# Transposes of a local-attention kernel in 64-token row tiles of the array, in place of 128x128

## The chip, the core and the metric

One core of one Trainium2 chip runs the program. TensorE (PE, with its weight loads listed as PEld), VectorE (DVE), ScalarE (ACT) and GpSimd (POOL) work at once and wait for each other through semaphores. The metric is device time in microseconds (us), the median of some runs.

## The reference

All arithmetic is float32. The input is x, 16 batches of 128 tokens with 128 features. A cross-attention block comes first. Then, for each of two layers, a local attention with 8 heads of 64 and a gated feed-forward part follow:

```python
h = shift_token(x)
q, k, v = split(h @ wqkv, 3)
q = l2norm(q) * qs;  k = l2norm(k) * ksc
q, k = rotary_xpos(q, k)
o = local_attention(q, k, v)     # window 64, looks one window back
x = x + o @ wo
h = layernorm(shift_token(x)) * lg + lb
h = h @ w1 + b1
a, g = split(h, 2)
x = x + (a * gelu(g)) @ w2 + b2
```

Since 128 tokens are two windows, the attention of a batch is a dense 128x128 score matrix of each head under one mask.

## The kernel before, in words

The change lies in the attention of the two layers. There the residual is kept transposed (features on partitions) in `xs`. A batch passes these steps:

- PE projects q, k and v (`qkv`, L386), each one 128x512 product into its own bank of PSUM. ACT squares q and k (L668), DVE sums the squares (L978), ACT turns them into factors (L672, L674). DVE multiplies by the rotary tables (L968, L971), POOL adds the two halves (L347) and scales k (L354). q and k of the batch now lie in `cs`, tokens on partitions.
- `rows_T` (L515): PE transposes q in four 128x128 pieces into bank TQ, and k in four into bank TK (L521). Each piece holds two heads. ACT copies bank TQ to `qT` (`q_rows`, L770), DVE copies bank TK to `kT` (`k_rows`, L997).
- `scores_` (L525): eight products with 64 rows each (L535), the two heads of a pair in the two halves of the array's rows.
- DVE applies factor and mask and finds the negated maxima (`maxima_`, L986, begun by a small MEMSET at L257 that waits for the scores), ACT takes the exponentials (`weights`, L757), DVE the reciprocals (L993), and POOL divides (L340). Even heads (a=0) and odd heads (a=1) are separate halves throughout.
- `weights_T` (L538): PE transposes the four weight matrices of a half, again into TQ (a=0) or TK (a=1) (L546). ACT copies each half to `pT` (`weights_out`, L762).
- `attend` (L549): products with v (L559), ACT copies the result (`heads_out`, L766), PE multiplies by wo (`out_proj`, L566), DVE adds it to `xs` (L1008), PE subtracts the mean (`deviation`, L571), ACT squares (L774), PE averages (`variance`, L575), ACT forms the factor (L778, L780) and DVE writes the normalised row (L1012).

The batches are software-pipelined by hand. `pipeline` calls on each engine a function `step`, in which at(d) is the batch n+d. The order of the calls in each `step` is the order in the engine's queue, and each engine works its queue in that order. In one step PE handles v and the transposes of batch n+2, the output product of batch n, q of batch n+4, mean and variance of batch n, the scores of n+2, the weight transposes and the attention product of n+1, and k of n+5. The weight transposes of the even half stand before `variance`, those of the odd half after the scores. In the same step ACT does the exponentials of n+1 with the copy of the heads of n between their halves, then the q copy of n+2, squares of k, the small functions, the copy of the even weights, squares of q, and the copy of the odd weights.

An fp32 product is two passes of the array, and so counts as two instructions in the trace; a transpose is one.

## Time and profile before

| | us |
|---|---|
| median of 3 runs (451.48 to 452.88) | 452.82 |
| span of the profiled execution | 452.5 |
| PE busy | 391.6 |
| DVE busy | 342.2 |
| ACT busy | 299.5 |
| POOL busy | 205.4 |

The profiled execution gives only its span, from the first to the last instruction; its own time outside the span isn't recorded. The span lies 0.3 us below the median of the runs. Busy times are sums over the whole span, which holds the cross-attention, two attention stages of 16 batches each and two feed-forward parts. The change touches the attention stages alone, so the views below are cut to them. Matmul ends are modelled, and neighbouring matmuls overlap, so that a busy PE isn't PE at its peak.

### The profile page before, as it was taken

What the parts mean: (1) busy time and instruction counts of PE and PEld (TensorE: products, weight loads), DVE (VectorE), ACT (ScalarE), POOL (GpSimd) and SP (SyncE); (2) the same over time, 40 slices, a digit from 0 to 9 for tenths busy, and PEclk for the clock granted to TensorE, in tenths of its full rate; (3) what the DMA queues carried; (4) which work ended last, traced back from release to release, by engine and by line L of the source; (5) the groups of instructions that cost most, each with busy time, mean ns of one, the idle gap of its engine ahead of it and who ended that gap; (6) DMA issues with size and microseconds to landing.
All of it is one profiled execution on the core that took longest, in us unless ns stands there. A gap on an engine that the chain in (4) does not pass through costs nothing.

```text
span 452.5 us, 8032 instructions
## 1 busy us (share of the span) xinstructions
PE 391.6 (87%) x2504; PEld 258.5 (57%) x2504; DVE 342.2 (76%) x1308; ACT 299.5 (66%) x986; POOL 205.4 (45%) x229
## 2 busy tenths in 40 slices
PE   0678677799999999987789888999999999867995
PEld 0456552477777767765434345767767777654442
DVE  2688747899999999984135689999999999612345
ACT  2355533589899899886432338889898998653224
POOL 6261103585775766762000066767757757410000
PEclk9988985999999999999989989999999999967898
DMA  7920000000000000000000000000000000000003
GB/s 158 292 55 2 1 1 0 0 3 1 1 2 2 0 2 1 3 0 1 0 1 0 1 0 2 0 3 2 2 0 1 3 1 1 2 1 0 0 0 93
DMA packets 10263, 7.25 MB, mean 16 GB/s; under 512 B 3245, under 2 KB 9431, under 8 KB 10222
## 3 DMA queue, kind: packets, MB, share of 16 engines
q1 hardware_dynamic: 8590, 5.63, 4.6%
q0 software_dynamic: 832, 1.12, 1.3%
q8 instruction: 20, 0.33, 0.3%
q14 instruction: 21, 0.17, 0.1%
q10 hardware_dynamic: 800, 0.00, 0.1%
HBM read 5.70 MB, written 1.05 MB: 15 GB/s over the span
## 4 chain that ended last, share of the span: by engine, by line
DVE 56%; PE 31%; issue 6%; ACT 4%; DMA 1%; SPq 0%; DVEq 0%; ACTq 0%
DVE pp L986 11%; PE ps L511 10%; DVE shared L971 8%; DVE ss L978 8%; DVE shared L968 7%; PE ps L618 5%; DVE kT L997 4%; PE ps L386 3%; DVE vv L1001 3%; DVE xs L1008 2%; PE ps L566 2%; PE ps L535 1%; DVE pri L993 1%; DVE nm L986 1%; DVE shared L872 1%
## 5 line engine op out<-in xcount | busy, mean ns | idle before, releaser
L386 PE MATMUL ps<-wqkv_raw,xs 128*128 128x512 f32 x192 | 108.2, 652 | 11.1 <-DVE shared L971 11.1
L340 POOL TENSOR_TENSOR pp<-pp,pri 128x512 f32<-128x512 f32 x64 | 66.6, 1041 | 94.8 <-DVE pri L993 94.8
L757 ACT ACTIVATE pp<-pp,nm 128x128 f32<-128x128 f32 x256 | 99.2, 389 | 10.3 <-DVE nm L986 10.3
L347 POOL TENSOR_TENSOR shared<-shared 128x512 f32<-128x512 f32 x64 | 81.4, 1275 | 0.0
L986 DVE CUSTOM_DVE_ANT_0 pp<-ps,msk,rr 128x128 f32<-128x128 f32 x256 | 72.4, 347 | 0.0
L511 PE MATMUL ps<-hn,w1g 128*128 128x512 f32 (+1 forms) x96 | 49.4, 637 | 5.8 <-DVE uu L1063 5.8
L757 ACT ACTIVATION_READ_ACCUMULATOR pp<-pp,nm 128x1 f32 x256 | 48.1, 188 | 0.0
L971 DVE TENSOR_TENSOR shared<-ps,stab 128x256 f32<-128x256 f32 x128 | 47.6, 413 | 0.0
L386 PEld LDWEIGHTS ps<-wqkv_raw,xs 128*128 128x128 f32 x192 | 31.1, 200 | 27.0 <-DVE shared L971 17.7
L968 DVE TENSOR_TENSOR shared<-ps,ctab 128x512 f32<-128x512 f32 x64 | 42.9, 671 | 2.5 <-ACT sqr L668 2.4
L559 PEld LDWEIGHTS ps<-pT,vv 128*64 128x64 f32 x512 | 28.2, 139 | 26.9 <-issue 24.1
L668 ACT ACTIVATE sqr<-ps 128x512 f32<-128x512 f32 x64 | 37.5, 586 | 8.7 <-PE ps L386 8.6
L1063 DVE SCALAR_TENSOR_TENSOR uu<-ps,b_all,gl 128x512 f32<-128x512 f32 (+1 forms) x24 | 17.6, 748 | 33.4 <-ACT gl L825 33.4
L978 DVE TENSOR_REDUCE ss<-sqr 128x8 f32<-128x512 f32 x64 | 40.7, 677 | 1.5 <-ACT sqr L668 1.5
L559 PE MATMUL ps<-pT,vv 128*64 128x128 f32 x512 | 35.9, 283 | 6.8 <-ACT pT L762 6.8
L546 PE MATMUL ps<-idn,pp 128*128 128x128 f32 x256 | 41.0, 284 | 0.1
L521 PEld LDWEIGHTS ps<-idn,shared 128*128 128x128 f32 x256 | 31.0, 141 | 17.3 <-issue 17.3
L825 ACT ACTIVATE gl<-ps,b_all 128x512 f32<-128x512 f32 (+1 forms) x24 | 16.0, 685 | 37.2 <-PE ps L511 37.2
L762 ACT ACTIVATE pT<-ps 128x512 f32<-128x512 f32 x64 | 37.5, 589 | 4.4 <-PE ps L546 4.4
L359 POOL TENSOR_SCALAR ssc<-ss 128x16 f32<-128x16 f32 x32 | 7.9, 246 | 69.6 <-DVE ss L978 69.6
L566 PE MATMUL ps<-oT,wo_raw 128*128 128x128 f32 x256 | 36.2, 287 | 3.6 <-ACT oT L766 3.6
L521 PE MATMUL ps<-idn,shared 128*128 128x128 f32 x256 | 37.7, 273 | 0.0
(118 smaller groups left out, 673.1 us busy)
## 6 DMA issues: line engine op xcount, KB each, us to landing
wqkv_raw<-in_L_ffn_wqkv_dram SPq DMA_DIRECT2D x1, 1536.0 KB, 16.4
out_dram<-shared SPq DMA_DIRECT2D x4, 256.0 KB, 2.5
w_raw<-in_L_ffn_w_dram SPq DMA_DIRECT2D x1, 682.0 KB
xt<-in_x_dram SPq DMA_DIRECT2D x2, 256.0 KB, 4.5
xt<-in_x_dram SPq DMA_DIRECT2D x1, 512.0 KB, 12.4
wo_raw<-in_L_ffn_wo_dram SPq DMA_DIRECT2D x1, 512.0 KB
ct<-in_ctx_dram POOLq DMA_DIRECT2D x1, 360.0 KB, 12.2
w_raw<-in_L_ffn_w_dram SPq DMA_DIRECT2D x2, 128.0 KB
```

What stands on the lines that cost most here:

```text
L340: T(pp[m.j][:, a, :, :], pp[m.j][:, a, :, :], pri[m.j][:, a * 4:a * 4 + 4].unsqueeze(2).to_broadcast([128, PAIRS, 128]), ALU.mult).then_in ...
L347: T(cs[m.j][:, part], cs[m.j][:, part], sn[m.j][:, part], ALU.add).then_inc((aq_done, ak_done)[s], 1)
L386: mm(ps[:, part, :], xs[:, m.b, 0:N], wqkv_raw[:, m.layer, part * INNER:(part + 1) * INNER], start=True, stop=True).then_inc((q_ps, k_ps, ...
L511: last = mm(ps[0:m, 2 * c + s, :], w1g[:, layer, o2:o2 + m], hg, start=True, stop=True)
L521: last = tr(ps[:, TQ + s, c * 128:(c + 1) * 128], cs[m.j][:, s * INNER + c * 128:s * INNER + (c + 1) * 128], idn[:])
L559: last = mm(ps[a * 64:a * 64 + 64, OB, c * 128:(c + 1) * 128], vv[m.j][:, h * DH:(h + 1) * DH], pT[m.j][:, a, c, :], start=True, stop=True)
L566: last = mm(ps[:, OB, Y], wo_raw[:, m.layer, c, :], oT[m.j][:, c, :], start=(c == 0), stop=(c == PAIRS - 1))
L757: A(pp[m.j][:, a, c, :], pp[m.j][:, a, c, :], ACT.Exp, bias=nm[m.j][:, a * 4 + c:a * 4 + c + 1], scale=-1.0, accum_out=psum_[m.j][:, a * 4 ...
L968: V.tensor_tensor(heads(cs[m.j], s), x_, ctab[:, m.layer, s, :].unsqueeze(1).to_broadcast([128, HEADS, DH]), ALU.mult)
L971: last = V.tensor_tensor(heads(sn[m.j], s)[:, :, o_], x_[:, :, i_], stab[:, m.layer, s, o_].unsqueeze(1).to_broadcast([128, HEADS, 32]), A ...
L978: V.tensor_reduce(ss[m.j][:, s * HEADS:(s + 1) * HEADS], heads(sqr[m.j], s), AX.X, ALU.add).then_inc(sq_sum, 1)
L986: last = V.tensor_tensor_reduce(out=pp[m.j][:, a, c, :], in0=ps[:, SA + a, c * 128:(c + 1) * 128], in1=msk[:], scale=rr[m.j][:, h:h + 1], ...
```

## The change

Each 128x128 transpose becomes two transposes of 64 tokens: one reads partitions 0 to 63, the other partitions 64 to 127 of the same piece (`row_tiles`). They use the two halves of the array's rows, and each writes 128x64 values: tokens 0 to 63 go to bank TQ, tokens 64 to 127 to bank TK. A bank thus holds no longer q or k (or even or odd heads), but one half of the tokens of all eight pieces. So:

- `rows_T` transposes q and k of a batch in one go of 16 instructions, after `out_proj`. It waits for both q and k from POOL. `q_rows` on ACT copies the lower tokens of q and k to the new tile `rT`, `k_rows` on DVE the upper ones. Both wait for the one semaphore `rT_ps`.
- `weights_T` transposes all eight weight matrices in one go of 16 instructions, after the scores. It waits for both halves from POOL. Both copies of `weights_out` wait for the one semaphore `pt_ps`.
- The copies write with a stride: eight runs of 64 values each.

```diff
--- before.py
+++ after.py
@@ -156,12 +156,12 @@
         cut = Carve()
         (cs0, sn0), (cs1, sn1) = ([cut(N, 2 * INNER) for _ in range(2)] for _ in range(2))
         cs, sn = (cs0, cs1), (sn0, sn1)
-        qT, kT = sb2("qT", [128, PAIRS, N]), sb2("kT", [128, PAIRS, N])
+        rT = sb2("rT", [128, 2 * PAIRS, N])
         vv = sb2("vv", [N, INNER])
         pp = [sb(f"pp{k}", [128, 2, PAIRS, 128]) for k in range(2)]
         zo = pp[1][:, 0, :, :]
         nm, psum_, pri = (sb2(n, [128, HEADS]) for n in ("nm", "psum_", "pri"))
-        pT = [sb(f"pT{k}", [128, 2, PAIRS, 128]) for k in range(2)]
+        pT = sb2("pT", [128, 2 * PAIRS, 128])
         oT = sb2("oT", [128, PAIRS, N])
         dsq, lnl, rstd = (sb(n, [D, N]) for n in ("dsq", "lnl", "rstd"))
 
@@ -202,10 +202,11 @@
         sqq_done, sqk_done, sq_sum, ss_ready, ln_done, r_ready = (
             sem(n) for n in ("sqq_done", "sqk_done", "sq_sum", "ss_ready", "ln_done", "r_ready"))
         tq_done, tk_done, aq_done, ak_done, mk_done = (sem(n) for n in ("tq_done", "tk_done", "aq_done", "ak_done", "mk_done"))
-        qT_ps, kT_ps, qT_ready, kT_ready, v_ready = (sem(n) for n in ("qT_ps", "kT_ps", "qT_ready", "kT_ready", "v_ready"))
+        rT_ps, lo_ready, hi_ready, v_ready = (sem(n) for n in ("rT_ps", "lo_ready", "hi_ready", "v_ready"))
         s_ps = sem("s_ps")
-        nm_done, p_done, ri_ready, pn_ready, pt_ps, pt_ready = (
-            sem2(n) for n in ("nm_done", "p_done", "ri_ready", "pn_ready", "pt_ps", "pt_ready"))
+        pt_ps = sem("pt_ps")
+        nm_done, p_done, ri_ready, pn_ready, pt_ready = (
+            sem2(n) for n in ("nm_done", "p_done", "ri_ready", "pn_ready", "pt_ready"))
         o_ps, oT_ready, y_ps, x_upd = (sem(n) for n in ("o_ps", "oT_ready", "y_ps", "x_upd"))
         m_ps, d2_ready, var_ps, lnl_done, rstd_ready, hn_ready = (
             sem(n) for n in ("m_ps", "d2_ready", "var_ps", "lnl_done", "rstd_ready", "hn_ready"))
@@ -512,39 +513,46 @@
                 if 1 in halves_:
                     last.then_inc(g_ps[c], 1)
 
-            def rows_T(m, s):
+            def row_tiles(t, bank, done):
+
+                for c in range(2 * PAIRS):
+                    for u, r in enumerate((slice(0, 64), slice(64, 128))):
+                        last = tr(ps[:, bank + u, c * 64:c * 64 + 64], t(c)[r, :], idn[r, r])
+                last.then_inc(done, 1)
+
+            def rows_T(m):
 
                 if m.b >= 2:
-                    pe.wait_ge(pt_ready[s], m.i - 1)
-                pe.wait_ge((aq_done, mk_done)[s], m.i + 1)
-                for c in range(PAIRS):
-                    last = tr(ps[:, TQ + s, c * 128:(c + 1) * 128],
-                              cs[m.j][:, s * INNER + c * 128:s * INNER + (c + 1) * 128], idn[:])
-                last.then_inc((qT_ps, kT_ps)[s], 1)
+                    pe.wait_ge(pt_ready[0], m.i - 1)
+                    pe.wait_ge(pt_ready[1], m.i - 1)
+                pe.wait_ge(aq_done, m.i + 1)
+                pe.wait_ge(mk_done, m.i + 1)
+                row_tiles(lambda c: cs[m.j][:, c * 128:(c + 1) * 128], TQ, rT_ps)
 
             def scores_(m):
 
-                pe.wait_ge(qT_ready, m.i + 1)
-                pe.wait_ge(kT_ready, m.i + 1)
+                pe.wait_ge(lo_ready, m.i + 1)
+                pe.wait_ge(hi_ready, m.i + 1)
                 if m.b > 0:
                     pe.wait_ge(nm_done[0], m.i)
                     pe.wait_ge(nm_done[1], m.i)
                 for c in range(PAIRS):
                     for a in range(2):
                         r = slice(a * 64, a * 64 + 64)
-                        last = mm(ps[:, SA + a, c * 128:(c + 1) * 128], qT[m.j][r, c, :], kT[m.j][r, c, :], start=True, stop=True)
+                        last = mm(ps[:, SA + a, c * 128:(c + 1) * 128], rT[m.j][r, c, :], rT[m.j][r, PAIRS + c, :], start=True, stop=True)
                 last.then_inc(s_ps, 1)
 
-            def weights_T(m, a):
+            def weights_T(m):
 
                 if m.b + 1 < B:
-                    pe.wait_ge((qT_ready, kT_ready)[a], m.i + 2)
-                else:
-                    pe.wait_ge(pt_ready[a], m.i)
-                pe.wait_ge(pn_ready[a], m.i + 1)
-                for c in range(PAIRS):
-                    last = tr(ps[:, TQ + a, c * 128:(c + 1) * 128], pp[m.j][:, a, c, :], idn[:])
-                last.then_inc(pt_ps[a], 1)
+                    pe.wait_ge(lo_ready, m.i + 2)
+                    pe.wait_ge(hi_ready, m.i + 2)
+                elif m.i > 0:
+                    pe.wait_ge(pt_ready[0], m.i)
+                    pe.wait_ge(pt_ready[1], m.i)
+                pe.wait_ge(pn_ready[0], m.i + 1)
+                pe.wait_ge(pn_ready[1], m.i + 1)
+                row_tiles(lambda c: pp[m.j][:, c // PAIRS, c % PAIRS, :], TQ, pt_ps)
 
             def attend(m):
 
@@ -557,7 +565,7 @@
                     for a in range(2):
                         h = 2 * c + a
                         last = mm(ps[a * 64:a * 64 + 64, OB, c * 128:(c + 1) * 128], vv[m.j][:, h * DH:(h + 1) * DH],
-                                  pT[m.j][:, a, c, :], start=True, stop=True)
+                                  pT[m.j][:, a * PAIRS + c, :], start=True, stop=True)
                 last.then_inc(o_ps, 1)
 
             def out_proj(m):
@@ -577,11 +585,10 @@
             def step(at, on):
                 if on(2):
                     project_v(at(2))
-                    rows_T(at(2), 0)
                 if on(0):
                     out_proj(at(0))
                 if on(2):
-                    rows_T(at(2), 1)
+                    rows_T(at(2))
                 if on(4):
                     project_q(at(4))
                 if on(0) and at(0).b == B - 3:
@@ -594,8 +601,6 @@
                     hidden(at(0).layer, 0, 1)
                 if on(0):
                     deviation(at(0))
-                if on(1):
-                    weights_T(at(1), 0)
                 if on(0) and not on(1):
                     hidden(at(0).layer, 0, 2, [0])
                 if on(0):
@@ -603,7 +608,7 @@
                 if on(2):
                     scores_(at(2))
                 if on(1):
-                    weights_T(at(1), 1)
+                    weights_T(at(1))
                 if on(5):
                     project_k(at(5))
                 if on(1):
@@ -758,16 +763,16 @@
                       scale=-1.0, accum_out=psum_[m.j][:, a * 4 + c:a * 4 + c + 1]).then_inc(p_done[a], 1)
 
             def weights_out(m, a):
-                act.wait_ge(pt_ps[a], m.i + 1)
-                A(pT[m.j][:, a, :, :].rearrange("p c n -> p (c n)"), ps[:, TQ + a, :], ACT.Copy).then_inc(pt_ready[a], 1)
+                act.wait_ge(pt_ps, m.i + 1)
+                A(pT[m.j][:, :, a * 64:a * 64 + 64], ps[:, TQ + a, :].rearrange("p (c n) -> p c n", n=64), ACT.Copy).then_inc(pt_ready[a], 1)
 
             def heads_out(m):
                 act.wait_ge(o_ps, m.i + 1)
                 A(oT[m.j][:].rearrange("p c n -> p (c n)"), ps[:, OB, :], ACT.Copy).then_inc(oT_ready, 1)
 
             def q_rows(m):
-                act.wait_ge(qT_ps, m.i + 1)
-                A(qT[m.j][:].rearrange("p c n -> p (c n)"), ps[:, TQ, :], ACT.Copy).then_inc(qT_ready, 1)
+                act.wait_ge(rT_ps, m.i + 1)
+                A(rT[m.j][:, :, 0:64], ps[:, TQ, :].rearrange("p (c n) -> p c n", n=64), ACT.Copy).then_inc(lo_ready, 1)
 
             def dev_square(m):
                 act.wait_ge(m_ps, m.i + 1)
@@ -963,7 +968,7 @@
 
                 dve.wait_ge((sqq_done, sqk_done)[s], m.i + 1)
                 if s == 1 and m.i >= 2:
-                    dve.wait_ge(kT_ps, m.i - 1)
+                    dve.wait_ge(rT_ps, m.i - 1)
                 x_, done = ps[:, QB + s, :].rearrange("p (h d) -> p h d", d=DH), (tq_done, tk_done)[s]
                 V.tensor_tensor(heads(cs[m.j], s), x_, ctab[:, m.layer, s, :].unsqueeze(1).to_broadcast([128, HEADS, DH]), ALU.mult)
                 for u in range(2):
@@ -993,8 +998,8 @@
                 V.reciprocal(pri[m.j][:, a * 4:a * 4 + 4], psum_[m.j][:, a * 4:a * 4 + 4]).then_inc(ri_ready[a], 1)
 
             def k_rows(m):
-                dve.wait_ge(kT_ps, m.i + 1)
-                V.tensor_copy(kT[m.j][:].rearrange("p c n -> p (c n)"), ps[:, TK, :]).then_inc(kT_ready, 1)
+                dve.wait_ge(rT_ps, m.i + 1)
+                V.tensor_copy(rT[m.j][:, :, 64:128], ps[:, TK, :].rearrange("p (c n) -> p c n", n=64)).then_inc(hi_ready, 1)
 
             def v_rows(m):
                 dve.wait_ge(v_ps, m.i + 1)
```

The first queue shown is that of PE, one step in the middle of an attention stage. `cs` is a part of the tile `shared`, and a product stands here as one row. Before:

```order
L386 MATMUL ps<-wqkv_raw,xs 128x512
L521 MATMUL ps<-idn,shared 128x128 x4
L566 MATMUL ps<-oT,wo_raw 128x128 x4
L521 MATMUL ps<-idn,shared 128x128 x4
L386 MATMUL ps<-wqkv_raw,xs 128x512
L571 MATMUL ps<-xs,cen 128x128
L546 MATMUL ps<-idn,pp 128x128 x4
L575 MATMUL ps<-dsq,ones 128x128
L535 MATMUL ps<-kT,qT 128x128 x8
L546 MATMUL ps<-idn,pp 128x128 x4
L386 MATMUL ps<-wqkv_raw,xs 128x512
L559 MATMUL ps<-pT,vv 64x128 x8
```

And the same step of PE now:

```order
L387 MATMUL ps<-wqkv_raw,xs 128x512
L574 MATMUL ps<-oT,wo_raw 128x128 x4
L520 MATMUL ps<-idn,shared 128x64 x16
L387 MATMUL ps<-wqkv_raw,xs 128x512
L579 MATMUL ps<-xs,cen 128x128
L583 MATMUL ps<-dsq,ones 128x128
L542 MATMUL ps<-rT 128x128 x8
L520 MATMUL ps<-idn,pp 128x64 x16
L387 MATMUL ps<-wqkv_raw,xs 128x512
L567 MATMUL ps<-pT,vv 64x128 x8
```

The q transposes moved from ahead of the output product (L566, now L574) to behind it, and the even weight transposes from ahead of the variance product (L575, now L583) to behind the scores.

The second queue is that of ACT, from the small functions of one step to the first exponentials of the next. Before:

```order
L778 ACTIVATE lnl<-ps,epst 128x128 [waits var_ps]
L780 ACTIVATE rstd<-lnl 128x128 [waits lnl_done]
L762 ACTIVATE pT<-ps 128x512 [waits pt_ps0]
L668 ACTIVATE sqr<-ps 128x512 [waits q_ps]
L762 ACTIVATE pT<-ps 128x512 [waits pt_ps1]
L757 ACTIVATE pp,psum<-pp,nm 128x128 [waits nm_done0]
```

And the same stretch of ACT now:

```order
L783 ACTIVATE lnl<-ps,epst 128x128 [waits var_ps]
L785 ACTIVATE rstd<-lnl 128x128 [waits lnl_done]
L767 ACTIVATE pT<-ps 128x8x64 [waits pt_ps]
L673 ACTIVATE sqr<-ps 128x512 [waits q_ps]
L767 ACTIVATE pT<-ps 128x8x64 [waits pt_ps]
L762 ACTIVATE pp,psum<-pp,nm 128x128 [waits nm_done0]
```

The order of ACT is the same. What the first copy waits for has changed: `pt_ps0` came with the even weight transposes ahead of the scores, `pt_ps` comes with all of them behind the scores.

## Rows read from the trace of the kernel before

**Rows 1.** The page, part 4: shares by engine of the chain that ended last.
```profile
DVE 56%; PE 31%; issue 6%; ACT 4%; DMA 1%; SPq 0%; DVEq 0%; ACTq 0%
```

**Rows 2.** Busy time by stretch: length, PE, PEld, DVE, ACT, POOL, clock, DMA share.
```profile
124.00:204.00 80.00, 78.18 (x635) 56.66 (x635) 77.64 (x319) 72.12 (x259) 55.38 (x58) 1.00 0.01 2
150.73:159.05 8.32, 8.32 (x68) 5.98 (x67) 8.22 (x33) 7.56 (x28) 5.76 (x7) 1.00 0.00 0
...
400.00:412.00 12.00, 9.60 (x40) 7.26 (x41) 1.63 (x6) 2.53 (x6) 1.04 (x1) 0.51 0.00 1
```

**Rows 3.** Timeline of one step: start, length in us, engine, line, operation, count.
```profile
150.73 0.06 DVE L257 MEMSET mark_v<- 128x1 f32 x1
...
151.98 0.40 ACT L757 ACTIVATE pp<-pp,nm 128x128 f32<-128x128 f32 x1 [0.18 <-DVE nm L986]
...
153.54 0.57 ACT L766 ACTIVATE oT<-ps 128x512 f32<-128x512 f32 x1
...
154.38 1.06 PE L566 MATMUL ps<-oT,wo_raw 128*128 128x128 f32 x8
...
155.27 0.60 PE L521 MATMUL ps<-idn,shared 128*128 128x128 f32 x4
...
155.47 0.61 DVE L1008 TENSOR_TENSOR xs<-ps,xs 64x128 f32<-64x128 f32 x2
155.56 0.57 ACT L770 ACTIVATE qT<-ps 128x512 f32<-128x512 f32 x1
...
155.71 1.03 PE L386 MATMUL ps<-wqkv_raw,xs 128*128 128x512 f32 x2
156.03 0.58 ACT L668 ACTIVATE sqr<-ps 128x512 f32<-128x512 f32 x1
...
156.57 0.38 PE L571 MATMUL ps<-xs,cen 128*128 128x128 f32 x2
...
156.99 0.28 ACT L774 ACTIVATE dsq<-ps 128x128 f32<-128x128 f32 x1 [0.38 <-PE ps L571]
...
157.32 0.49 PE L575 MATMUL ps<-dsq,ones 128*128 128x128 f32 x2
...
157.74 1.16 PE L535 MATMUL ps<-kT,qT 64*128 64x128 f32 x16
...
158.25 0.31 ACT L780 ACTIVATE rstd<-lnl 128x128 f32<-128x128 f32 x1
158.47 0.58 ACT L762 ACTIVATE pT<-ps 128x512 f32<-128x512 f32 x1
158.77 0.28 DVE L1012 TENSOR_TENSOR hn<-ps,rstd 128x128 f32<-128x128 f32 x1
...
158.84 0.66 PE L546 MATMUL ps<-idn,pp 128*128 128x128 f32 x4
...
159.05 0.06 DVE L257 MEMSET mark_v<- 128x1 f32 x1
...
159.33 1.02 PE L386 MATMUL ps<-wqkv_raw,xs 128*128 128x512 f32 x2
...
159.53 0.60 ACT L762 ACTIVATE pT<-ps 128x512 f32<-128x512 f32 x1
```

**Rows 4.** Instructions of a line, 124 to 204 us: ns least/median/most, first and last start.
```profile
L546 PE MATMUL ps<-idn,pp x77: 272/273/328, 123.8 to 200.5; 128*128 128x128 f32 x77
...
L535 PE MATMUL ps<-kT,qT x160: 272/272/373, 124.5 to 200.0; 64*128 64x128 f32 x160
...
L546 PEld LDWEIGHTS ps<-idn,pp x76: 137/141/146, 125.5 to 200.4; 128*128 128x128 f32 x76
...
L535 PEld LDWEIGHTS ps<-kT,qT x160: 182/188/188, 124.4 to 199.8; 64*128 64x128 f32 x160
```

**Rows 5.** The same view of the 16 normalised rows of each layer.
```profile
L1012 DVE TENSOR_TENSOR hn<-ps,rstd x16: 277/278/292, 100.2 to 224.8; 128x128 f32<-128x128 f32 x16
...
L1012 DVE TENSOR_TENSOR hn<-ps,rstd x16: 276/278/292, 285.2 to 414.5; 128x128 f32<-128x128 f32 x16
```

## The prediction

> **What bounds the kernel now.** Start with the chain that ended last. It gives 56% to DVE and 31% to PE, hardly any to ACT [rows 1]. That suggests DVE as the bound, so read the busy times of a stretch in the middle of an attention stage next. In 80 us PE is busy 78.18, DVE 77.64, ACT 72.12, and the granted clock is 1.00, the 2.4 GHz level [rows 2]. Two engines are full and the third nearly so. Which of them sets the pace can't be told from sums, so take one step in order of time [rows 3]. I count it from one MEMSET mark_v to the next, 150.73 to 159.05, 8.32 us. This MEMSET is the DVE instruction that waits for the scores.
>
> The timeline shows a ring that passes through all three engines. Scores end at 157.74+1.16 = 158.90, DVE starts at 159.05. DVE's first maxima release the first exponential of ACT, 1.25 us behind the MEMSET (151.98), and ACT did wait there (0.18, released by DVE). The copy of the heads follows on ACT at 153.54. It ends at 154.11 and releases the output product (154.38). PE then works through k transposes (155.27), q of a later batch (155.71) and deviation (156.57). ACT's square waits for it (0.38 idle, start 156.99). The variance (157.32) waits for the square, and the scores (157.74) follow it. In between, DVE's addition to the residual starts at 155.47, just when the output product ends (154.38+1.06 = 155.44).
>
> So the step is a ring with little slack anywhere. The important sign for this change is where the copies of the transposed weights stand on ACT. The even one starts at 158.47, before the scores are done. The odd one starts at 159.53, 0.48 behind the MEMSET, and is the last thing on ACT ahead of the exponentials.
>
> **The price of a pair of row tiles.** Full transposes follow each other in (0.60-0.27)/3 = 0.109 us (L521 at 155.27). The new ones stream 64 columns instead of 128, so 0.055 for a pair if both halves of the array work at once and the weight load hides. That halves do work at once is seen in the scores: 16 passes of 64 rows in 1.16 us, of which 0.10 is a long first pass (373 ns against 272, rows 4), so (1.16-0.27-0.10)/7 = 0.112 per pair, as much as one full pass. Whether 128 weight columns load in 0.055 has to be bounded. After a switch the first pass is as much longer as its weights take to load: 373-272 = 0.101 us for the scores, but 328-273 = 0.055 for a transpose. The loads' own durations say the same (188 against 141 ns) [rows 4]. So load and stream would just match, and the upper end is 0.109, if they can't overlap or if instructions can't be issued at twice the rate. I take 0.06, near the lower end because of the 0.055 row, and keep 0.109 for the range.
>
> The Trainium skill (TensorE: Matmul & The Clock Gate, LDWEIGHTS) gives a load as the weight columns divided by 1.2 GHz, whatever the number of rows: 107 ns for 128 columns, so halving the rows would save nothing and a pair would cost as much as a full transpose. The trace agrees for the scores (0.101) and disagrees for transposes (0.055). By the rule the second rival below would be the forecast.
>
> **The price of changing between row tiles and the full array.** The variance ends at 157.32+0.49 = 157.81, so its last pass started at 157.54. The first scores start at 157.74 and are 0.10 long, so in effect at 157.84, 0.30 behind. Without a change the next pass follows after 0.11 (q's at 155.71 behind k's last). A change therefore costs 0.20 where full weights load, and behind the scores, where the last pair starts at 158.90-0.27 = 158.63 and the transposes in effect at 158.84+0.055 = 158.90, it costs 0.16. A transpose next to a product of the same tiling costs nothing extra, as the 154.38 to 155.71 stretch shows. The Trainium skill (TensorEngine Tiling (Array Packing), Key Properties) states that a change of mode drains TensorE. The trace agrees, with these 0.16 to 0.20 us.
>
> **The change part by part, along the ring of one step.**
> 1. Weight transposes and ACT. All 16 stand behind the scores now. They start 0.11 behind the scores' last pair (same tiling, no change): 158.74. The last of 8 pairs starts at 158.74+7x0.06 = 159.16 and ends at 159.43. ACT follows 0.03 after an end of PE, as DVE did at 155.47: 159.46. This is the first copy, which before was at 158.47, under cover of the scores. The spacing of such a copy to the next operation is 0.47 (155.56 to 156.03), and the squares of q stand between the two copies, so the second copy is at 159.46+0.94 = 160.40 and the exponentials can start at 160.87. That is 1.82 behind the MEMSET, against 1.25 to 1.30 before: I take +0.54. DVE's maxima were late; now ACT itself is late. The copies' stride costs nothing in my sum: there is no row of it in this stage, and I allow 0.1 us each for the range.
> 2. Output product. It follows the copy of the heads, so +0.54. Before, the q transposes held it up: heads done 154.11, output product at 154.38. After a wait for ACT a product starts in effect 0.16 behind (square done 157.27, variance at 157.32 plus a 0.10 longer first pass). So it could have started 0.10 earlier, and moving q away gives that back: +0.44.
> 3. Output product to q. Before, 155.71-154.38 = 1.33. Now 8 passes of 0.112 = 0.89, a change 0.16, 8 pairs 0.48, a change back 0.20: 1.73, so +0.40. Halving the transposes' time is eaten here by the two changes and by q's four, which were off the ring.
> 4. From q to the next MEMSET. The even weight transposes no longer stand between deviation and variance, but they were hidden behind ACT's square (156.99 to 157.27, variance at 157.32): 0.
> 5. The copies of q and k. Both wait for the last pair. With q's projection at 155.71+0.84 = 156.55, that pair starts 0.26 before (0.06 + 0.20) at 156.29 and ends at 156.56. ACT copies at 156.59 and squares until about 157.6. The square of the deviation is due at 156.99+0.84 = 157.83, so it hides, with 0.2 to spare. On DVE the residual comes 0.44 later and the k copy also waits for the last pair, some 0.05 more. DVE's last normalised row would be ready at 158.77+0.5 = 159.27, but waits for its factor (158.56+0.84 = 159.40, row at 159.43). It takes 0.28, and the scores come at 159.05+0.84 = 159.89 for DVE: hidden.
> 6. PE behind the weight transposes. k's projection follows at 159.16+0.06+0.20 = 159.42, 0.1 later than before, and attention waits for the second copy, done at 160.40+0.60 = 161.0. PE idles some 0.8 us, but the heads are copied by ACT only in its order, at 160.87+1.56: hidden, as attention, 16 passes like the scores' 1.16 us, ends by 162.4.
>
> Sum: 0.44+0.40 = 0.84 us per step, 8.32 to 9.16. A layer has 14 steps with both an output product and new scores. I count 13, because at a layer's start the ring isn't closed yet. 26 x 0.84 = 21.8 us. The profiled span of 452.5 would become 474.3. It lies 0.3 below the median of the runs, 452.82, so 474.6; I say 475.
>
> **The rivals.**
> - Pairs cost 0.109. Then term 3 grows by 8x0.049 = 0.39 and term 1 by 7x0.049 = 0.34: 0.73 more per step, 19 us, so 494. For it: no row shows two loads and two passes in less than 0.109. Against: the 0.055 load after a switch.
> - PE has the last word and the change is no slower. PE is busy in all 8.32 us of the step [rows 2]. It gives up 16x0.109 = 1.74 and takes 16x0.06 = 0.96, and changes cost +0.16+0.20 around rows and -0.16+0.20 around weights: 0.38 less. DVE has 8.22 busy in a step, so at most 0.1 could be had: -2.6, 450. The place is ACT's first exponential. If it starts within 1.3 us of the MEMSET the ring isn't lengthened there. That needs both weight copies ready 0.5 us earlier than I find. Against: ACT works in order, and its first copy can't start before the scores end.
> - The clock falls. PE gets holes of 0.8 us, and in the sparse end of the second layer the clock was 0.51, the 1.2 GHz level, while the same stretch of the first layer kept it. That layer took 414.5-285.2 = 129.3 us against 124.6 [rows 5]: 4.7 us for one such fall [rows 2]. Two of them on top of the forecast: 484. Against: PE would still be busy some nine tenths of each step.
>
> **How the numbers follow.** Forecast 0.66: 475, own range 466 to 484 (a change that costs nothing between transposes and products takes off 0.2 to 0.36 a step, up to 9 us; strides or a pair of 0.075 add as much). Pairs at 0.109: 0.18, at 494. Clock: 0.09, at 484. PE's rival: 0.05, at 450. Rest 0.02. To hold 8 in 10 the range takes the forecast's own, the clock's case and half of the second rival: 466 to 494. A measurement of this kernel tells about 0.3% (1.4 us) from no change. Faster 0.04, the same 0.03, slower 0.93.
>
> **What would show it.** In the profile after: MEMSET to MEMSET 9.1 to 9.2 us in mid-layer; the first pT copy 0.4 behind the MEMSET and released by PE; the first exponentials 1.8 behind it and no longer released by DVE; the output product 4.1 behind it, against 3.65; 1.7 us from there to q's projection; 16 transposes in about 0.8 us; DVE idle ahead of the residual; attention waiting for pT. It is wrong if the exponentials still wait for DVE, or if 16 transposes take over 1 us.

## The result, and the profile after

The changed kernel took 475.64 us (median of 4 runs, 473.53 to 480.5), the kernel before 452.15 (4 runs, 450.89 to 452.88). The ratio is 1.0528, interval 1.0473 to 1.0583: 23.5 us slower. The profiled execution took 476.09 us, its span is 474.3, so 1.8 us lie outside the span. Span against span it is 474.3 - 452.5 = 21.8 us. Here and below a median is over all executions, while ratios and intervals leave out those in a slower state, over 1.5% above the fastest of their kernel.

The page of the changed kernel, part 4: shares by engine of the chain that ended last.
```profile
PE 67%; ACT 15%; DVE 12%; issue 3%; DMA 1%; POOL 1%; SPq 0%; DVEq 0%; ACTq 0%
```
This answers [rows 1]. DVE fell from 56% to 12%, ACT rose from 4% to 15%. In mid-layer the chain now holds no DVE; PE and ACT hand the work to each other. In the kernel before, the chain of one mid-layer step (150.7 to 159.2 us) is DVE alone:
```profile
by line: DVE pp L986 24.7%; DVE shared L971 15.5%; DVE ss L978 14.0%; DVE shared L968 13.8%; DVE kT L997 8.1%; issue 7.7%; DVE vv L1001 6.8%; DVE xs L1008 4.2%; DVE pri L993 3.1%; DVE nm L986 2.5%; DVE hn L1012 1.5%; DVE mark_v L257 1.4%
```

Busy time by stretch after (length, PE, PEld, DVE, ACT, POOL, clock, DMA share, GB/s): mid-layer, one step, and the sparse ends of the two layers, where the last batches run without new ones behind them.
```profile
124.00:204.00 80.00, 69.34 (x711) 47.32 (x711) 74.17 (x292) 65.77 (x236) 49.70 (x52) 1.00 0.01 2
163.06:172.25 9.19, 8.12 (x90) 5.52 (x87) 8.50 (x34) 7.57 (x27) 5.76 (x7) 1.00 0.00 1
221.00:235.00 14.00, 10.63 (x55) 7.75 (x56) 1.64 (x7) 4.47 (x15) 2.08 (x2) 0.53 0.00 0
420.00:434.00 14.00, 10.08 (x66) 7.12 (x63) 1.94 (x9) 5.48 (x20) 2.08 (x2) 0.76 0.01 1
```
The end of the first layer in the kernel before, which [rows 2] doesn't show:
```profile
211.00:225.00 14.00, 10.11 (x72) 6.56 (x68) 2.88 (x16) 7.18 (x27) 2.08 (x2) 1.00 0.00 0
```
Against [rows 2]: the step grew from 8.32 to 9.19 us. PE is now idle 1.07 in each, DVE 0.69, at a clock of 1.00. ACT does the same 7.57 us of work (7.56 before). PE's busy time even fell, from 8.32 to 8.12 us. So the added time is waiting, not work.

Timeline of that step after (start, length, engine, line, operation, count, idle before and its releaser), answering [rows 3].
```profile
163.06 0.06 DVE L258 MEMSET mark_v<- 128x1 f32 x1 [0.17 <-PE ps L542]
...
163.44 0.60 ACT L767 ACTIVATE pT<-ps 128x512 f32<-128x512 f32 x1 [0.88 <-PE ps L520]
...
164.41 0.60 ACT L767 ACTIVATE pT<-ps 128x512 f32<-128x512 f32 x1
...
164.89 0.41 ACT L762 ACTIVATE pp<-pp,nm 128x128 f32<-128x128 f32 x1
...
165.16 1.09 PE L567 MATMUL ps<-pT,vv 128*64 128x128 f32 x16 [0.70 <-ACT pT L767]
...
166.19 1.12 PE L387 MATMUL ps<-wqkv_raw,xs 128*128 128x512 f32 x2
...
166.43 0.59 ACT L771 ACTIVATE oT<-ps 128x512 f32<-128x512 f32 x1
...
167.15 1.08 PE L574 MATMUL ps<-oT,wo_raw 128*128 128x128 f32 x8
...
168.16 0.71 PE L520 MATMUL ps<-idn,shared 64*128 64x64 f32 x16
...
168.81 1.12 PE L387 MATMUL ps<-wqkv_raw,xs 128*128 128x512 f32 x2
...
172.25 0.06 DVE L258 MEMSET mark_v<- 128x1 f32 x1 [0.17 <-PE ps L542]
```
Counted from the MEMSET: first exponential +1.83 (1.25 before), output product +4.09 (3.65), q's projection +5.75 (4.98), next MEMSET +9.19 (8.32). The new thing is the 0.70 us for which PE waits, ahead of the attention products, for ACT's second copy. In the kernel before, attention started 1.23 behind the MEMSET (150.73), against 2.10 now:
```profile
151.96 1.09 PE L559 MATMUL ps<-pT,vv 128*64 128x128 f32 x16
```

The row-tiled transposes of this kernel, 124 to 204 us (ns least/median/most, first and last start), answering the transposes of [rows 4].
```profile
L520 PEld LDWEIGHTS ps<-idn,pp x144: 137/138/140, 125.9 to 199.9; 64*128 64x128 f32 x144
L520 PE MATMUL ps<-idn,pp x144: 216/222/223, 126.0 to 199.9; 64*128 64x64 f32 x144
...
L520 PE MATMUL ps<-idn,shared x128: 221/223/272, 131.4 to 196.2; 64*128 64x64 f32 x128
```
One takes 222 ns from start to end where a full transpose took 273. In the group of the weights (`pp`) no first pass is longer, since none takes over 223 ns; in that of q and k (`shared`) the first takes 272. 16 took 0.66 us with the weights and 0.71 with q and k. That bounds a pair at (0.66-0.22)/7 = (0.71-0.22-0.05)/7 = 0.063 us. Some 0.01 of each group is the start of the second of a pair behind the first. By the single starts in the trace, the first and the last of 8 pairs of the weights start at 162.747 and 163.174, so a pair is 0.427/7 = 0.061 us.

The normalised rows of both layers, answering [rows 5].
```profile
L1017 DVE TENSOR_TENSOR hn<-ps,rstd x16: 292/292/293, 98.3 to 238.0; 128x128 f32<-128x128 f32 x16
...
L1017 DVE TENSOR_TENSOR hn<-ps,rstd x16: 291/292/293, 298.3 to 436.3; 128x128 f32<-128x128 f32 x16
```
139.7 and 138.0 us, against 124.6 and 129.3. The starts of the first maxima of each batch split the span (before, after): start to first maxima 84.5, 82.0; layer one, first to last maxima 125.1, 135.9; between the layers 60.0, 63.1; layer two 125.1, 136.9; rest 57.8, 56.4. The attention stages grew by 10.8 and 11.8, 22.6 together. The rest is -2.5, +3.1 and -1.4, which leaves the 21.8. The change touches little of the rest. At the start, where 2.5 us were saved, the granted clock differs: it was 0.68 in 60 to 70 us and 0.50 in 70 to 80 before, 0.84 and 0.75 after.

### The profile page after: what moved, and what is told of

It is laid out like the page before. It is cut to its first block, busy times and chain, and to the rows that moved or that the text cites. A ratio compares the mean times of both kernels' runs of the same rounds, so it can differ in the third digit from the quotient of the medians.

```text
span 474.3 us, 9060 instructions
## 1 busy us (share of the span) xinstructions
PE 381.0 (80%) x3016; PEld 244.1 (51%) x3016; DVE 348.6 (74%) x1308; ACT 299.0 (63%) x986; POOL 205.2 (43%) x229
## 3 DMA queue, kind: packets, MB, share of 16 engines
q0 software_dynamic: 832, 1.12, 1.1%
## 4 chain that ended last, share of the span: by engine, by line
PE 67%; ACT 15%; DVE 12%; issue 3%; DMA 1%; POOL 1%; SPq 0%; DVEq 0%; ACTq 0%
PE ps L387 14%; PE ps L512 9%; PE ps L520 8%; ACT pT L767 7%; PE ps L567 7%; PE ps L574 7%; PE ps L542 7%; PE ps L623 5%; PE ps L583 3%; ACT sqr L673 3%; ACT dsq L779 2%; PE ps L579 2%; DVE shared L877 1%; DMA wo_s<-in_L_xattn_Wo_dram 1%; DVE ss L983 1%
## 5 line engine op out<-in xcount | busy, mean ns | idle before, releaser
L387 PE MATMUL ps<-wqkv_raw,xs 128*128 128x512 f32 x192 | 110.5, 663 | 12.9 <-DVE shared L976 12.9
L567 PEld LDWEIGHTS ps<-pT,vv 128*64 128x64 f32 x512 | 29.7, 142 | 47.9 <-issue 46.5
L762 ACT ACTIVATION_READ_ACCUMULATOR pp<-pp,nm 128x1 f32 x256 | 51.0, 199 | 0.0
L387 PEld LDWEIGHTS ps<-wqkv_raw,xs 128*128 128x128 f32 x192 | 30.6, 196 | 30.3 <-DVE shared L976 18.6
L574 PEld LDWEIGHTS ps<-oT,wo_raw 128*128 128x128 f32 x256 | 33.0, 201 | 20.8 <-ACT oT L771 20.8
L574 PE MATMUL ps<-oT,wo_raw 128*128 128x128 f32 x256 | 37.3, 292 | 3.0 <-ACT oT L771 3.0
L542 PE MATMUL ps<-rT 64*128 64x128 f32 x512 | 38.1, 289 | 0.0
L1013 DVE TENSOR_TENSOR xs<-ps,xs 64x128 f32<-64x128 f32 x64 | 18.5, 289 | 26.3 <-PE ps L574 25.2
```

What stands on the lines that cost most here:

```text
L387: mm(ps[:, part, :], xs[:, m.b, 0:N], wqkv_raw[:, m.layer, part * INNER:(part + 1) * INNER], start=True, stop=True).then_inc((q_ps, k_ps, ...
L542: last = mm(ps[:, SA + a, c * 128:(c + 1) * 128], rT[m.j][r, c, :], rT[m.j][r, PAIRS + c, :], start=True, stop=True)
L567: last = mm(ps[a * 64:a * 64 + 64, OB, c * 128:(c + 1) * 128], vv[m.j][:, h * DH:(h + 1) * DH], pT[m.j][:, a * PAIRS + c, :], start=True, ...
L574: last = mm(ps[:, OB, Y], wo_raw[:, m.layer, c, :], oT[m.j][:, c, :], start=(c == 0), stop=(c == PAIRS - 1))
L762: A(pp[m.j][:, a, c, :], pp[m.j][:, a, c, :], ACT.Exp, bias=nm[m.j][:, a * 4 + c:a * 4 + c + 1], scale=-1.0, accum_out=psum_[m.j][:, a * 4 ...
```

## The experiments

Each ratio is against the kernel before, run on the same chip. "Step" is the time from MEMSET to MEMSET in mid-layer, from each kernel's own profile. It is known far better than the whole time, because the clock at the ends of layers moves that by several us. Line numbers differ by a few between kernels; the tiles' names tell what a row is.

**Which part costs, and is it its tiles or its place?** Four kernels. rows_tiled tiles and moves only the transposes of q and k, weights_tiled only those of the attention weights. The other part is as before.
```diff
 # rows_tiled: step() after the change, with the weights' old calls
                 if on(0):
                     deviation(at(0))
+                if on(1):
+                    weights_T(at(1), 0)
...
-                    weights_T(at(1))
+                    weights_T(at(1), 1)
 # weights_tiled: step() after the change, with the rows' old calls
                     project_v(at(2))
+                    rows_T(at(2), 0)
                 if on(0):
                     out_proj(at(0))
                 if on(2):
-                    rows_T(at(2))
+                    rows_T(at(2), 1)
```


> Only the q and k transposes are in row tiles, all 16 behind the output product; the weight transposes and their copies are those of the kernel before. Ring theory: the output product starts 0.10 earlier, since the q transposes no longer stand ahead of it, and q's projection stands 1.76 behind the output product instead of 1.33. Net +0.33 per step, 26 steps, +8.6 us: 461. Step 8.65. Rival (all of the loss comes from ACT's late weight copies): the rows cost nothing, 452 to 453. Rival (the loss is that of the changes of tiling alone, 0.36 per step here): 461 too, told apart by rows_late.

Measured: 459.1 us, 1.0131 (1.0077 to 1.0185), step 8.61: +0.29, as expected. The output product came 3.43 behind the MEMSET, 0.22 earlier than before, and q's projection 1.73 behind it, 0.40 later. The missing 0.10 is the longer first pass of q's projection (1.12 against 1.03 us). The exponentials stayed at +1.25. So the rival by which the rows cost nothing is out.

> Only the weight transposes are in row tiles, all 16 behind the scores; q and k as in the kernel before. Ring theory: ACT's first exponential goes from 1.28 to 1.83 behind the MEMSET, the output product from 3.65 to 4.09; between it and the scores nothing changes. Step +0.44, 8.77, 26 steps, +11.4 us: 464. With rows_tiled the two parts then make up 20 of the 23 us lost. Rival (the loss lies in the rows): 452 to 453.

Measured: 479.52 us, 1.058 (1.0514 to 1.0647), step 9.20. A clear miss: the weights alone cost 0.88 a step, twice the 0.44 of the sum, and as much as the whole change. The chain of waits of one step (start, us, what) shows why.
```profile
153.85 0.45 PE ps L520 x13
154.30 0.02 issue
154.33 0.60 ACT pT L769
154.92 0.49 ACT sqr L675
155.41 0.50 ACT pT L769
155.91 0.14 issue
156.04 1.09 PE ps L568 x16
157.14 1.06 PE ps L387 x2
158.19 0.44 PE ps L529 x4
158.63 0.89 PE ps L575 x8
```
It doesn't go through ACT's exponentials and the copy of the heads. It goes from the second weight copy to the attention products (L568), v's projection (L387), q's transposes (L529) and only then to the output product (L575), all in PE's own order. The heads had been copied at 157.90, 0.57 before the output product started (158.47). Attention starts 2.10 behind the MEMSET, as in the changed kernel, and the output product 2.43 behind attention. In the kernel before that was 154.38-151.96 = 2.42: there, too, PE went from attention to the output product without a wait, and the whole +0.88 is attention's later start.

The same two parts again, moved, but left as full 128x128 transposes.
```diff
 # rows_late: before, with
                     project_v(at(2))
-                    rows_T(at(2), 0)
                 if on(0):
                     out_proj(at(0))
                 if on(2):
+                    rows_T(at(2), 0)
                     rows_T(at(2), 1)
 # weights_late: before, with
-                if on(1):
-                    weights_T(at(1), 0)
...
                 if on(1):
+                    weights_T(at(1), 0)
                     weights_T(at(1), 1)
```


> Full 128x128 transposes as before, but those of q moved behind the output product, next to those of k. Ring theory: 0.10 given back at the output product, four transposes of 0.109 more between it and q's projection, net +0.34 per step, +8.8 us: 461, the same as rows_tiled, since halving the transposes' time just pays the two changes of tiling. Rival (only the changes of tiling cost): no change or a gain, 450 to 453.

Measured: 466.32 us, 1.0307 (1.0239 to 1.0376), step 8.64. The step is that of rows_tiled (8.61) within 0.03: half the transposing time of q and k buys nothing, since the two changes of tiling take it. From the output product to q's projection it is 155.99-154.12 = 1.87 us here with no change of tiling on the way, and 1.73 in rows_tiled, or 1.83 with its 0.10 of longer first pass. The rival, that only the changes cost, is out. Of the 7 us more in the whole time 5.7 are in the sparse end of the first layer. First rows_tiled, then rows_late:
```profile
214.00:228.00 14.00, 10.25 (x72) 6.70 (x72) 2.88 (x16) 7.18 (x27) 2.08 (x2) 1.00 0.00 0
```
```profile
215.00:229.00 14.00, 11.60 (x48) 8.77 (x49) 1.62 (x6) 3.85 (x14) 1.68 (x2) 0.51 0.00 0
```
The granted clock was 1.00 (2.4 GHz) in the one and 0.51 (1.2 GHz) in the other. Between the last maxima of layer one and the first of layer two rows_tiled took 59.7 us, rows_late 65.4.

> Full 128x128 transposes as before, but the four of the even weights moved from ahead of the variance product to behind the scores; each half keeps its own semaphore. Ring theory: the first copy starts 0.48 behind the MEMSET instead of 0.58 ahead of it, the exponentials about 1.89 behind it; +0.5 per step, +13 us: 465, the same within 2 us as weights_tiled. So the place costs, not the tiles. Rival (row tiles or the strided copies are what is dear): no change, 452 to 453.

Measured: 474.07 us, 1.0464 (1.0405 to 1.0524), step 9.29. So it is the place of the weight transposes that costs (0.97), and the tiles give 0.09 of it back. The size was missed as in weights_tiled, for the same cause; its chain has the same links. The rival, that the tiles or the strided copies are dear, is out. In the whole time it is 5 us faster than weights_tiled, with a longer step. Its clock stood at 1.00 in 221 to 235 us, where weights_tiled had 0.52, and between the layers it took 4.4 us less.

**Is it ACT's order?** after_swap and before_swap change one thing in the kernels after and before: ACT squares q ahead of both weight copies instead of between them. weights_tiled_swap has the same edit in weights_tiled.
```diff
+                if on(4):
+                    squares(at(4), 0)
                 if on(1):
                     weights_out(at(1), 0)
-                if on(4):
-                    squares(at(4), 0)
                 if on(1):
                     weights_out(at(1), 1)
```


> The changed kernel with one edit: ACT squares q ahead of the two weight copies instead of between them, in the 0.9 us in which it waits for the transposes. Ring theory: the second copy follows the first, ACT's first exponential goes from 1.83 to 1.32 behind the MEMSET (DVE allows 1.28), the output product from 4.09 to 3.65, step 9.19 to 8.74, 26 x 0.45 = 11.7 us less: 464. Rival (PE's transposes and changes of tiling carry the loss, ACT has slack): 475, unchanged.

Measured: 465.31 us, 1.0269 (1.0237 to 1.0301), step 8.70, so 0.49 of the 0.87 comes back. Its timeline:
```profile
159.11 0.06 DVE L258 MEMSET mark_v<- 128x1 f32 x1 [0.17 <-PE ps L542]
...
159.50 1.08 ACT L767 ACTIVATE pT<-ps 128x512 f32<-128x512 f32 x2 [0.39 <-PE ps L520]
...
160.47 0.40 ACT L762 ACTIVATE pp<-pp,nm 128x128 f32<-128x128 f32 x1
...
160.73 1.09 PE L567 MATMUL ps<-pT,vv 128*64 128x128 f32 x16 [0.21 <-ACT pT L767]
```
ACT idled 0.39 for the transposes instead of 0.88, and exponentials and attention both came 0.47 to 0.48 sooner behind the MEMSET (1.36 for 1.83, 1.62 for 2.10). The size was a hit, but not for the reason expected: the chain of waits runs from the second copy through attention and v's projection to the output product, and the exponentials aren't in it.

> The kernel before with the same edit on ACT. Ring theory: no change, 452, since the even copy has slack there and the odd copy is released by PE at 0.48 behind the MEMSET either way. Rival (squares of q ahead of the copies help in themselves): 2 us or more less.

Measured: 453.33 us, 1.0017 (0.9993 to 1.0041), step 8.32. No change, as expected: where the transposes come early enough, the order of the squares is free.

> weights_tiled (row tiles for the weights alone, behind the scores) with ACT's squares of q ahead of the copies. Ring theory: first exponential at 1.32 instead of 1.83, which is what the kernel before has within 0.05, output product at 3.65; step 8.32 to 8.36, so 452 to 454. PE has about 0.4 us more to spare in each step, which gains nothing as long as the ring is what it is. Rival (PE was the bound of the kernel before): 2 us less, 450, where DVE's 8.22 of busy time stops it.

Measured: 466.8 us, 1.0313 (1.0284 to 1.0343), step 8.71. A miss. With the exponentials early I expected nearly all of the loss to go, but here too the chain runs second copy, attention, v, q's transposes, output product:
```profile
160.06 1.09 ACT pT L769 x2
161.15 0.14 issue
161.29 1.09 PE ps L568 x16
162.38 1.05 PE ps L387 x2
163.44 0.44 PE ps L529 x4
163.87 0.22 PE ps L575 x2
```

dev_first is weights_tiled_swap with the deviation's product ahead of q's projection in mid-layer.
```diff
+                if on(0) and at(0).b < B - 4:
+                    deviation(at(0))
                 if on(4):
                     project_q(at(4))
...
-                if on(0):
+                if on(0) and at(0).b >= B - 4:
                     deviation(at(0))
```


> weights_tiled_swap with the deviation product ahead of the projection of q in all steps but the last four of a layer, so that ACT's square and the variance no longer stand behind that projection. Ring theory: deviation waits for DVE's addition (ends 0.64 behind the output product), then q's projection covers ACT's square; the scores come 0.1 to 0.15 earlier, until DVE's own 8.22 us are the bound: step 8.24 to 8.3, 1 to 2 us less than the kernel before, 450 to 451. Rival (DVE sets the step already): no change, 452.

Measured: 466.49 us, 1.0269 (1.0221 to 1.0317), step 8.60. The 0.1 a step of this edit came (8.60 for 8.71); the level missed, as in weights_tiled_swap, from which it was reckoned.

**Is it v behind attention?** The last four move v's projection of a later batch ahead of the attention products, so that it fills PE's wait. In the kernels without the swap this should take one link out of the chain. weights_tiled_v, after_v and weights_tiled_swap_v are the named kernels with the edit, best_v is dev_first with it.
```diff
 # PE, step(): v one batch earlier, ahead of attend
-                    project_v(at(2))
...
                     project_k(at(5))
+                if on(3):
+                    project_v(at(3))
 # DVE, v_rows: its buffer is still read by attention two batches back
                 dve.wait_ge(v_ps, m.i + 1)
+                if m.b >= 2:
+                    dve.wait_ge(o_ps, m.i - 1)
```


> weights_tiled with the projection of v for the next batch ahead of the attention product, in the 0.7 us in which PE waits there for the second weight copy, instead of between the attention product and the q transposes (and one more wait on DVE that keeps the v tile safe). Revised theory (weights_tiled is bound by a second branch of the ring, second copy, attention, v, q transposes, output product, at 4.52 behind the MEMSET): taking v's 1.0 us out of the branch brings the output product to 4.1, where ACT's exponentials and the copy of the heads hold it; step 9.20 to 8.78, 26 x 0.42 = 11 us less, 468 to 469. Rival (ACT's late exponentials were the whole story, or something else on DVE holds the step): 479, unchanged.

Measured: 467.22 us, 1.0341 (1.0284 to 1.0397), step 8.79: a hit in both. Its chain:
```profile
160.56 0.60 ACT pT L770
161.16 0.49 ACT sqr L676
161.65 0.49 ACT pT L770
162.13 1.52 ACT pp L765 x8
163.65 0.50 ACT oT L774
164.15 0.04 issue
164.19 1.16 PE ps L575 x8
```
With v out of the way the step falls by 0.41. It is 0.47 above the kernel before, where item 2 of the prediction gives 0.44, and the chain is that item's path: exponentials, copy of the heads, output product. That confirms the cause of the weights_tiled miss by taking it away.

> The changed kernel with the same move of v's projection. Revised theory: there the branch through attention and v (166.29 + 0.86 = 167.15) and the branch through the exponentials and the heads (copy ends 167.02, output product at 167.15) end within 0.1 us of each other, so shortening one gives at most 0.1: step 9.1 to 9.19, 473 to 476. Rival (only the branch through attention binds): step 8.8, 10 us less.

Measured: step 9.19, as in the changed kernel, and a chain through the exponentials and heads as in weights_tiled_v: a hit. The whole time tells less and gives no ratio. The median is 481.08 us; one execution took 473.16 at a mean clock of 0.959, the other three 480.99 to 481.22 at 0.928 to 0.932. In the changed kernel, then, taking away the path over v gives nothing: both paths end together.

> weights_tiled_swap (squares of q ahead of the copies) with the move of v. Revised theory: both branches are shortened. The exponentials start 1.32 behind the MEMSET as in the kernel before; PE now has k's and v's projections and then attention ahead of the q transposes, output product at about 3.73; step 8.71 to 8.4, 8 us less than 467, 459. Rival (the two branches aren't what binds): 467.

> The same with the deviation product ahead of q's projection in all steps but the last four of a layer. Revised theory: 0.1 per step less again, 8.3, level with the kernel before or just under it in mid-layer; the time stays 2 to 5 us over it where the clock falls at the sparse end of the first layer, as in dev_first: 455 to 458. If it doesn't fall there, 452 to 453.

Measured: 466.81 us, 1.0341 (1.0275 to 1.0408), step 8.75, and 466.89 us, 1.0286 (1.0219 to 1.0353), step 8.65. Both missed and gained nothing over the same kernels without the edit. The chain of weights_tiled_swap_v:
```profile
151.10 0.44 PE ps L520 x14
151.54 1.91 PE ps L387 x4
153.45 1.05 PE ps L568 x16
154.50 0.02 issue
154.52 0.61 ACT oT L774
155.13 0.04 issue
155.17 1.16 PE ps L575 x8
```
PE now does k's and v's projections in a row (1.91 us) before attention. With the swap the weight copies are ready earlier than that, so attention is late for v's sake, the heads are late for attention's, and the output product stands where it stood. What the move can bring is bounded by PE's wait ahead of attention that v fills: 0.71 us in weights_tiled, 0.22 in weights_tiled_swap. None of the twelve beats the kernel before; the nearest that carries a part of the change is rows_tiled.

## Why the prediction was right, and where its reasons were not

The time (475 for 475.64), the sign and the checkpoints came out. One step of the reasoning was wrong, and the sum hid it. That the time fits to 1 us is in part luck.

- **The ring has no slack: not shown by the rows, but borne out.** The rows of the kernel before show DVE full as well, and its mid-layer chain is DVE alone. A ring with slack under a full DVE would have swallowed a part of the loss. The runs left none: +0.29 in rows_tiled for 0.33 expected, +0.47 in weights_tiled_v for 0.44, and the MEMSET stands 0.15 behind the end of the scores in both kernels (158.90 to 159.05 before, 172.10 to 172.25 after).
- **Price of a pair: right.** 0.061 us measured, 0.06 taken. The rival at 0.109 (first in the list, called the second in the text) is out. The argument from first passes wasn't: a first pass was said to be longer by the load of its weights, but the same transposes have a first pass of 216 ns behind the scores and 272 behind the output product. The rule of the Trainium skill (TensorE: Matmul & The Clock Gate, LDWEIGHTS), 107 ns for 128 weight columns whatever the rows, would have held a pair to that; the trace of the changed kernel disagrees, with 0.061 for a pair.
- **Changes of tiling: right in sum.** Output product to q measured 168.81-167.15 = 1.66, and 1.76 with the 0.10 by which q's first pass is longer (1.12 against 1.03 [rows 3]); 1.73 was predicted.
- **Item 1, ACT: right.** First copy +0.38 (0.41), first exponential +1.83 (1.82).
- **Item 2, output product: right in time, wrong in reason.** It came at +4.09, as forecast. The item and **item 6** said that only the copy of the heads decides this, and that attention, waiting for the second copy, is hidden. Item 6 is the step that failed. It counted attention's own 1.1 us and stopped. It left out v's projection, which PE does next, ahead of the output product; in the kernel before q's transposes (0.44) stand there too. Attention starts 2.10 behind the MEMSET now and 1.23 before: +0.87. That is the whole of the +0.88 of weights_tiled, where q's transposes stay on this path and item 2 would give 0.44.
- **Why the sum was right all the same: luck.** Moving q's transposes behind the output product takes 0.44 out of that second path: 0.88 - 0.44 = 0.44, the very number of the path over the heads. In the changed kernel the two end together: the heads are ready at 166.43+0.59 = 167.02, and with the 0.16 of item 2 a product can start in effect at 167.18; v's projection starts at 166.19 and PE passed on 0.96 behind such a start before (152.98 to 153.94), so it comes to the output product at 167.15, which is when it started. From the first weight copy to the output product's end the chain takes 4.79 us in the changed kernel and in after_v alike. after_v (no gain) and weights_tiled_v (-0.41) show it from both sides. The parts don't add: weights +0.88, rows +0.29, together +0.87. By the terms of the sum they would be +0.44 and +0.30, so the rows were right and the weights off by a factor of two.
- **Item 3: right** (+0.43 with the longer first pass). rows_late adds that its halved transposes bring nothing.
- **Items 4 and 5: right.** From q's projection to the MEMSET 3.44, less the same 0.10, is 3.34, as before. The residual came later and held nothing up. The strided copies cost at most 10 ns: 599 ns on ACT against 589 for the flat copies of the weights before, 691 against 691 on DVE.
- **26 steps: right by the whole, not by its parts.** The two stages grew by 22.6 us, which is 26 x 0.87. In the traces ten steps of each layer grew by 0.87, and the other five by 2.2 us together in the first and 3.2 in the second. Outside the stages the span lost 0.8 us (-2.5, +3.1, -1.4), which the sum knew nothing of. It cancelled the 0.8 by which the stages grew more than forecast.
- **PE has the last word, at 450: out.** It asked for exponentials within 1.3 of the MEMSET. after_swap got them to 1.36 and still took 465.31, because of attention and v's projection.
- **The clock, at 484: the fall came, its price not.** Before, the clock stood at 1.00 at the end of layer one and fell to 0.51 at that of layer two [rows 2]; after, it fell to 0.53 at the end of layer one, and was 0.76 over 14 us at that of layer two, a part of them at the lower level. So layer one has a new fall, and the stretch between the layers grew by 3.1 us. But the start and the end got shorter by 3.9. In mid-layer the clock was 1.00 in spite of PE's 0.7 us holes.
- The prediction set the span (452.5) 0.3 below the median. That compared a span with whole times, and the 1.8 us outside were not reckoned. Span to span it was 474.3 against 474.3, and that close only because the 0.8 us above cancelled.

## What to carry to other kernels

Where a wait is added on an in-order engine, follow everything queued behind the waiting instruction to the next hand-over, not only that instruction: in weights_tiled 1.5 us of v's projection and q's transposes stood between attention and the output product, and with them a wait that was called hidden set the step. A sum for a change of two parts can be right while one part is wrong by a factor of two; only one part alone on the chip shows it. Halving an operation's time gained nothing here, where it had to be gathered behind its last input, and one reordered instruction of the engine that waits (here ACT's squares, 0.49 of 0.87 us) can be worth more than the faster operation.

## What the runs showed of the hardware that was not expected

- **Transposes in two row tiles run at 1.8 times the rate of full ones**: 0.061 us for a pair of 64-row fp32 transposes (0.062 in the group of q and k), against 0.109 for a full one. Two loads of 128 weight columns fit into these 0.061 us. A load took 138 ns from start to end, a single transpose 222.
- **The first pass of a group isn't always longer.** Behind the scores, of the same tiling, the row-tiled transposes begin at 216 ns; behind the output product, of the full array, at 272.
- **The clock at a layer's sparse end is not the same from kernel to kernel.** Some 14 us at 0.51 to 0.53 came in rows_late, weights_tiled and the changed kernel, not in rows_tiled and weights_late at the same place, though PE was busy over 10 of 14 us in all of them (where the clock was low, at that clock). Between the layers the kernels with the fall took 5.7 us more (rows_late 65.4, rows_tiled 59.7) and 4.4 (weights_tiled 65.3, weights_late 60.9); the changed kernel took 63.1 and the kernel before 60.0. Why one falls and another not was not tried and stays open.
- **The scatter between executions of one kernel goes with the mean clock.** The changed kernel took 473.53 at a mean clock of 0.956 and 480.5 at 0.929, with the same code. Seven executions of the kernel before ran from 450.9 us at 0.954 to 456.26 at 0.94. One of best_v took 496.92 us at 0.81, the other three 463.1 to 467.71 at 0.926 to 0.944. A step read in mid-layer at a clock of 1.00 tells apart what the whole time doesn't: rows_tiled and rows_late have one step and differ by 7 us.
